# Keeping V on the chip, one K buffer per batch, queries stored once, first heads loaded behind the stores (layers 1 and 4), and a feed-forward with its factors four times

## What is computed

```
# attention of layers 1 and 4, for each batch and head
q = split_heads(ln(x) @ Wq.T + bq) ; k = split_heads(ctx @ Wk.T + bk) ; v = split_heads(ctx @ Wv.T + bv)
p = softmax(q @ k.T / sqrt(8), masked)                 # 256 x 1601
x = x + merge_heads(p @ v) @ Wo.T + bo

# feed-forward of layer 4, rank 32, inner width 512
P = ln(x) @ U1                                         # 128 -> 32
H = gelu(P @ V1 + b1)                                  # 32 -> 512
x = x + (H @ U2) @ V2 + b2                             # 512 -> 32 -> 128
```

## Time and profile before

| | |
|---|---|
| Median of 3 runs | 2220.75 us (2220.43 to 2221.65) |
| The profiled execution's own time | 2221.38 us |
| Its span in the trace | 2219.6 us |
| TensorE busy | 1937.4 us, 87% |
| VectorE busy | 1311.8 us, 59% |
| ScalarE busy | 1287.8 us, 58% |
| DMA queue of SP | 60673 packets, 99.71 MB, 15.0% of 16 engines |

### The profile page before, as it was taken

One profiled execution on the slowest core, in us unless ns is written; L12 is line 12 of the kernel. 1 busy time (PEld: TensorE's weight loads), 2 busy tenths in 40 slices (PEclk: granted clock), 3 DMA queues, 4 the chain that ended last, 5 costly groups with the idle time before them and its releaser, 6 DMA issues. The chain is left out here.

```text
span 2219.6 us, 43657 instructions
## 1 busy us (share of the span) xinstructions
PE 1937.4 (87%) x17168; PEld 1364.1 (61%) x17168; DVE 1311.8 (59%) x3235; ACT 1287.8 (58%) x2062; POOL 130.5 (6%) x352
## 2 busy tenths in 40 slices
PE   5799999956839459999999999999993599999997
PEld 4577777733715356777777777777761356666663
DVE  5688888867446325455455455545546576666652
ACT  3699999943319114555555555555552366666662
POOL 3000000000014110000000000000000300000000
PEclk9899999976959679999999999999995789999996
DMA  7312111101061330000000000000001721112110
GB/s 264 115 54 57 55 54 54 49 16 68 1 174 33 111 113 1 1 1 1 1 1 2 1 1 1 1 2 1 2 1 57 252 68 53 53 56 61 51 32 14
DMA packets 62490, 107.27 MB, mean 48 GB/s; under 512 B 11241, under 2 KB 36541, under 8 KB 62289
## 3 DMA queue, kind: packets, MB, share of 16 engines
q1 hardware_dynamic: 60673, 99.71, 15.0%
q0 software_dynamic: 1616, 4.79, 0.7%
HBM read 75.09 MB, written 29.36 MB: 47 GB/s over the span
## 5 line engine op out<-in xcount | busy, mean ns | idle before, releaser
L2406 ACT ACTIVATE a_prT<-bank 128x512 f32<-128x512 f32 (+1 forms) x448 | 232.7, 565 | 328.3 <-PE bank L2315 328.0
L1212 DVE CUSTOM_DVE_ANT_0 a_attn_junk<-wide,a_mask 128x801 f32<-128x801 f32 (+1 forms) x256 | 247.5, 991 | 124.8 <-PE wide L1043 124.3
L1155 ACT ACTIVATE a_attn_prT<-bank 128x512 f32<-128x512 f32 (+1 forms) x448 | 237.3, 566 | 122.4 <-PE bank L1060 109.7
L2431 DVE CUSTOM_DVE_ANT_0 a_sc<-wide,a_zeros 128x1024 f32<-128x1024 f32 (+1 forms) x256 | 243.1, 987 | 91.9 <-PE wide L2301 91.9
L1501 DVE CUSTOM_DVE_ANT_0 a_attn_sc<-wide,a_mask 128x801 f32<-128x801 f32 (+1 forms) x256 | 252.8, 988 | 14.4 <-PE wide L1355 12.7
L1371 PE MATMUL bank<-ident,a_attn_sc 128*128 128x128 f32 x1664 | 244.4, 275 | 15.2 <-ACT a_attn_prT L1460 14.1
L1371 PEld LDWEIGHTS bank<-ident,a_attn_sc 128*128 128x128 f32 x1664 | 198.1, 141 | 62.6 <-issue 42.5
L2315 PE MATMUL bank<-ident,a_sc 128*128 128x128 f32 x1664 | 231.3, 277 | 1.5 <-ACT a_prT L2406 1.5
L2315 PEld LDWEIGHTS bank<-ident,a_sc 128*128 128x128 f32 x1664 | 185.4, 141 | 54.4 <-issue 28.1
L1466 ACT ACTIVATE a_attn_sc<-a_attn_sc,a_attn_nmx 128x1601 f32<-128x1601 f32 x128 | 209.6, 1638 | 5.7 <-DVE a_attn_nmx L1507 5.6
L2301 PE MATMUL wide<-a_kT,a_qT 64*128 64x512 f32 (+1 forms) x1024 | 211.0, 529 | 0.0
(11 more groups left out here) (456 smaller groups left out, 2561.5 us busy)
## 6 DMA issues: line engine op xcount, KB each, us to landing
a_ks<-a_k_parts SPq DMA_DIRECT2D x384, 75.0 KB
a_k_parts<-a_proj_kp SPq DMA_DIRECT2D x24, 416.0 KB, 5.3
a_v_rows<-a_proj_vb SPq DMA_DIRECT2D x8, 936.0 KB, 6.2
a_vs<-a_v_rows SPq DMA_DIRECT2D x32, 234.0 KB
a_q_stack<-a_proj_qp SPq DMA_DIRECT2D x18, 256.0 KB, 3.8
a_qx<-a_q_stack SPq DMA_DIRECT2D x128, 36.0 KB
moe_w1b<-in_e_w SPq DMA_DIRECT2D x15, 256.0 KB, 2.8
ctxT<-in_ctxT SPq DMA_DIRECT2D x4, 832.0 KB, 10.9
```

The lines of the kernel that those rows point to most:

```text
L1155: act.activation(prT[0:keys, u % PRT, kt:kt + m, :], bank_of(s, f"W{g}")[0:keys, 0:m * S].rearrange("p (t q) -> p t q", q=S), ACT.Exp).the ...
L1212: dve.tensor_tensor_reduce(junk[:, n % 2, 0:w], S_WIDE[n % 2][:, 0:w], mask(qt, at, w), 1.0, LOWEST, ALU.add, ALU.max, mx[:, p % 2, qt, e, ...
L2406: copy = lambda out, src: act.activation(out, src, ACT.Copy)
L2431: dve.tensor_tensor_reduce(sc[:, s % 2, h, at:at + w], S_WIDE[h][:, 0:w], zeros[:, 0:w], 1.0, LOWEST, ALU.add, ALU.max, mx[:, s % 2, h, p: ...
```

## The change

Layers 1 and 4:

- V is copied out of PSUM straight into `vs`, which now holds all four batches and 16 heads, and stays there. `vb`, the V stores, the V loads and TensorE's wait for them are gone. The ones beside V are set by GpSimd (one memset of 832 elements in each partition), not by VectorE (416).
- `kp` has a buffer for each of the four batches; ScalarE's wait for stores is gone.
- Each query part is stored once (three stores, not nine); the load of a head repeats it three times, with one DMA for each part. A head takes six DMAs instead of four.
- The heads 0 and 1 are loaded at the end of the projection block, behind the last K stores on SP, once the stores of the queries and of batch 0 have landed; the attention begins with head 2.

Layer 4's feed-forward: U1 comes four times side by side, so `pT` holds four copies at partitions 0, 32, 64 and 96. V1's four pieces lie at these four, and each matmul of a half uses its own 32 rows of the array and its own bank. The U2 matmuls no longer accumulate: each writes its own 32 partitions of one bank, and V2, four times below itself, sums the four in a contraction over 128. Signals are now one for each half, and a half is finished before the next one's U2 matmuls.

```diff
 def project_stage(...)
-        kp = core.sb(ctx, name + "_kp", [P, 2, 3, cols], BF16)
-        vb = core.sb(ctx, name + "_vb", [P, 2, HEADS, kts * VCOLS], F32)
+        kp = core.sb(ctx, name + "_kp", [P, blocks, 3, cols], BF16)
...
         def _(sp):
             sp.wait_ge(qpart3, 2)
             for j in range(3):
-                for i in range(3):
-                    sp.dma_start(q_rows(j, i), qp[:, j, :]).then_inc(q_stored, 16)
+                sp.dma_start(q_rows(j), qp[:, j, :]).then_inc(q_stored, 16)
             for i in range(blocks):
-                sp.wait_ge(v_evac, ng * (i + 1))
-                sp.wait_ge(ones_in, 1)
-                sp.dma_start(v_rows(i), vb[:, i % 2, :, :]).then_inc(v_stored[i], 16)
                 sp.wait_ge(part3, n_ck * (i + 1))
                 for rows, j in k_rows(i):
-                    sp.dma_start(rows, kp[:, i % 2, j, :]).then_inc(k_stored[i], 16)
-            sp.wait_ge(q_stored, 16 * 9)
+                    sp.dma_start(rows, kp[:, i, j, :]).then_inc(k_stored[i], 16)
+            sp.wait_ge(q_stored, 16 * 3)
+            sp.wait_ge(k_stored[0], 16 * len(k_rows(0)))
+            load_first(sp)
...
             def first_part(n):
-                if i >= 2 and n % n_ck == 0:
-                    act.wait_ge(k_stored[i - 2], 16 * len(k_rows(i - 2)))
...
         def _(pool):
+            pool.memset(vs[:, :, :, :].rearrange("p k h (t d) -> p (k h t) d", d=VCOLS)[:, :, 8:9], 1.0).then_inc(ones_in, 1)
...
         def _(dve):
-            dve.memset(vb[:, :, :, :].rearrange("p k h (t d) -> p (k h t) d", d=VCOLS)[:, :, 8:9], 1.0).then_inc(ones_in, 1)
...
-                        if i >= 2 and c == 0:
-                            dve.wait_ge(v_stored[i - 2], 16)
-                        out = vb[:, i % 2, :, kt * VCOLS:(kt + size) * VCOLS].rearrange(...)
+                        out = vs[:, i, :, kt * VCOLS:(kt + size) * VCOLS].rearrange(...)
 def masked_head_layer(...)
+        def load(sp, b, h, k, sem):
+            for j in range(3):
+                sp.dma_start(ks[24 * j:24 * (j + 1), k, 0:SC],
+                             k_parts[b, h, :, :, 0:SC].rearrange("i d c -> (i d) c")).then_inc(sem, 16)
+            for j in range(3):
+                sp.dma_start(qx[24 * j:24 * (j + 1), k, :],
+                             q_stack[h, j, :, b * S:(b + 1) * S].unsqueeze(0).broadcast_to([3, 8, S])).then_inc(sem, 16)
+        def load_first(sp):
+            for h in range(LOADED_AHEAD):
+                load(sp, 0, h, h, loaded[h])
...
-            sp.dma_start(qx[0:STACK, k, :], q_stack[h, :, :, :, b * S:(b + 1) * S].rearrange("j i d c -> (j i d) c")).then_inc(sem, 16)
 def row_quad_stage(...), quad_attention_stage(...)
-            for u in range(UNITS):
+            for u in range(LOADED_AHEAD, UNITS):
...
-                    pe.wait_ge(v_loaded[q % V_RING], 16 * (q // V_RING + 1))
 def ffn3_stage(...)
+        p_bank, h_bank = bank[0:2], (bank[2:6], bank[6:8] + bank[0:2])
+        q_bank, o_bank = bank[2:4], bank[4:6]
+        rows = lambda i: slice(i * RANK, (i + 1) * RANK)
...
             for c in range(2):
                 pe.wait_ge(p_out, c + 1)
                 for i in range(NC):
-                    if c:
-                        pe.wait_ge(gelu_done, i + 1)
-                    pe.matmul(bank[2 + i][:, :], v1[:, i * P:(i + 1) * P], pT[:, half(c)],
-                              start=True, stop=True).then_inc(h_ready, 1)
+                    ins = pe.matmul(h_bank[c][i][:, :], v1[rows(i), :], pT[rows(i), half(c)], start=True, stop=True)
+                ins.then_inc(h_ready, 1)
             for c in range(2):
                 pe.wait_ge(gelu_done, NC * (c + 1))
                 for i in range(NC):
-                    ins = pe.matmul(bank[c][0:RANK, :], u2[:, i, :], hT[:, c, i, :], start=(i == 0), stop=(i == NC - 1))
+                    ins = pe.matmul(q_bank[c][rows(i), :], u2[:, i, :], hT[:, c, i, :], start=True, stop=True)
                 ins.then_inc(q_ready, 1)
-            for c in range(2):
                 pe.wait_ge(q_out, c + 1)
```

More of the change, by code:

```diff
@@ L893, in _ @@
             for c in range(2):
-                pe.matmul(bank[c][0:RANK, :], u1, core.xnT[:, half(c)], start=True, stop=True).then_inc(p_ready, 1)
+                pe.matmul(p_bank[c][:, :], u1, core.xnT[:, half(c)], start=True, stop=True).then_inc(p_ready, 1)
             for c in range(2):
@@ L960, in quad_attention_stage @@
      recip_done, normed, mixed, mixed_out, out_ready, added, setup) = (core.sem(f"{name}_{s}") for s in names)
-    loaded = [core.sem(f"{name}_loaded{i}") for i in range(RING)]
-    v_loaded = [core.sem(f"{name}_v_loaded{i}") for i in range(V_RING)]
     S_WIDE, BANKS, U_BANK = core.wide, core.bank[0:3], core.bank[3]
@@ L1036, in score_piece @@
                 if n == 0:
-                    pe.wait_ge(loaded[s % RING], 64 * (s // RING + 1))
+                    pe.wait_ge(loaded[s % RING], 96 * (s // RING + 1))
                 if 4 * s + n >= 2:
@@ L1559, in project_stage @@
     k_stored = [core.sem(f"{name}_k_stored{i}") for i in range(blocks)]
-    v_stored = [core.sem(f"{name}_v_stored{i}") for i in range(blocks)]
     K_BANK, V_BANK, Q_BANK = core.bank[0:3], core.bank[3:6], core.bank[6:8]
@@ L1725, in masked_head_layer @@
         qx = q_words[:, :].bitcast(BF16).rearrange("p (s c) -> p s c", s=RING)
-        vs = sb("vs", [P, V_RING, 4, KT * VCOLS])
+        vs = sb("vs", [P, B, HEADS, KT * VCOLS])
+        loaded = [core.sem(f"{name}_loaded{i}") for i in range(RING)]
         mask_in = core.sem(name + "_mask_in")
```

83 lines of the change are left out of this document (32 added, 51 removed).

## The result

| | changed kernel | before, same chip |
|---|---|---|
| median | 2189.1 us (4 runs, 2186.7 to 2189.7) | 2221.2 us (4 runs, 2220.4 to 2224.4) |
| profiled execution | 2189.70 us, span 2187.9 | 2221.38 us, span 2219.6 |

What follows compares the result with a forecast made beforehand. Stores were taken to bound layer 1's projections (layer 4 has the same stages), TensorE the last feed-forward. 17.5 (layer 1) + 13.9 (layer 4) + 15.0 (feed-forward) = 46.4 us gained, giving 2174.4 us; range 2168 to 2183.

Steps and rivals of the forecast that it cites:

- ScalarE's wait goes, the last stores come 13.04 us earlier.: Layer 1's projections: without the wait for K stores, batch 3 and the last K stores come 13.04 us earlier, at 43.0.
- Three took 1.14 us, with the gaps between them I take 0.4 each, 4.8 in all.: End of the projections: SP issues twelve loads before the block can end, 0.4 us each, 4.8 in all.
- the change of block: From projections to attention: 0.5 us allowed, a choice between 0 and 1.
- The bound of 13 for layer 1: Layer 1's projections, forecast gain 17.5 us: lower bound, no gain beyond the 13.04 us by which the last stores move.
- its bound of 11: Layer 4's projections: lower bound of the forecast gain of 13.9 us; the upper was 15.5.
- Layer 4: VectorE's memsets late next: Layer 4's attention start: VectorE's memsets end 2.05 us after the block opens, and its first maximum can't come before.
- Edits at nothing: Layers 1 and 4: memset moved to GpSimd, six DMAs a head; taken as 0, bounds -0.4 to +0.8 us.
- rival 4: Attention of both layers: heads' loads fall behind, slower than before; 2302 us at 1 us per unit; chance 0.03.
- The feed-forward, 15.0: Last feed-forward: packed V1 and U2 matmuls gain 15.0 us if TensorE's clock is at its upper level by 2195.
- rivals 1 and 3: Feed-forward: TensorE's clock stays low, 2178.2 us, chance 0.20; strips of 32 rows don't run together, 2186.6 us, chance 0.06.
- the reason given for the clock: Feed-forward: it goes like layer 1's projections, which begin with two matmuls of U1's shape; upper level before U2, 8 us in.
- rival 1: Feed-forward: TensorE's clock stays at its lower level, 3.8 us more, 2178.2 us; chance 0.20.

Runs made afterwards that it cites:

- after_again: The changed kernel run once more with no edit; 2190.1 us (5 runs, 2185.0 to 2190.9).
- mask_last: The changed kernel with the whole mask work of layers 1 and 4 behind VectorE's last chunk of the last batch; 2185.7 us.
- one_q_load: The changed kernel, but queries stored three times and each loaded with one DMA of 72 rows; 2180.2 us, ratio 0.981.
- ahead1: The changed kernel with only the first head, not two, loaded ahead of the attention block; 2180.4 us, ratio 0.981.
- ff_only: The kernel before with the new last feed-forward alone, nothing changed in layers 1 and 4; 2206.3 us, ratio 0.9925.
- ff_u1_wide_v1_narrow: The changed kernel with the old feed-forward, U1 at 128 columns, V1's matmuls reading 32 rows as before; 2198.8 us, one run.
- ff_first_product_wide: The changed kernel with the old feed-forward, U1 at 128 columns and V1 padded with zeros to 128 rows; 2190.8 us, one run.

## Why the prediction was wrong, step by step

1. **ScalarE's wait goes, the last stores come 13.04 us earlier.** Right in kind. 43.97 instead of 43.0 in layer 1, and 43.23 in after_again, so most of that 1.0 is scatter. In layer 4 the last parts are 1.7 us late, counted from the stage's own start, because batch 3 waits behind the mask instructions (mask_last: 2.7 us of that layer).
2. **"Three took 1.14 us, with the gaps between them I take 0.4 each, 4.8 in all."** This step failed. The price of a key load in an empty queue was put on the query loads, whose form was new, and on loads queued behind stores. Measured 8.7 and 8.4 us: 2.2 of the difference from query loads at 0.69 instead of 0.36 us, 1.6 from the first three behind the stores. one_q_load and ahead1 take SyncE's time away in two different ways, and each gives back 9 us of the kernel's time, 8.4 and 7.3 of it in the two layers' profiles. The sum for layer 1: 1.0 for the parts, 3.9 for the loads, 0.3 for the change of block (0.75 instead of 0.5), and 5.2 is what TensorE's start missed (55.65 for 50.4). In layer 4 it is 1.7 for the parts, 3.6 for the loads and 0.4 for stores and block, and VectorE's first maximum is 5.6 us late; the attention behind it took 0.9 us less than before.
3. **The range.** The bound of 13 for layer 1 let the last stores move and nothing else; it did not hold issue at the largest price that a row shows for one (1815 ns in the old load's row above). 12.4 was measured at TensorE's start and 11.7 at the stage's end; layer 4's 9.1 lies below its bound of 11 too. Even the execution that lost nothing in the untouched stages, 2185.0 us in after_again, lies above the range.
4. **Layer 4: VectorE's memsets late next.** Right: TensorE starts at 1756.80, and the first maximum follows the memsets at 1758.72, 2.0 us after the block's opening.
5. **Edits at nothing.** Right in the main: the attention took 0.7 us longer in layer 1, inside the bounds of -0.4 to +0.8, and 0.9 less in layer 4, outside them. The cover for six DMAs a unit held: in all of both layers TensorE waits for a query load once each, at the start. So rival 4 (slower) did not come.
6. **The feed-forward, 15.0.** Right in size, 15.2, and in ff_only too; rivals 1 and 3 failed. But the reason given for the clock does not hold. I argued from the projections' two matmuls "of the very shape that U1 now has". ff_u1_wide_v1_narrow has them, and the clock stayed at 0.50 for 18 us behind them. So the size was right by luck in this part: if my reading of the strips holds, it was V1's place on four strips that kept rival 1 away, which the argument didn't use. No run shows that.
7. **What nobody had in the sum:** the untouched stages, 4.3 us. after_again shows that it is which way an execution goes, not the change. Its profile gained 36.4 us, 12.6 + 8.7 + 15.2 and -0.1 between. Whether the new start times make the costly way likelier is open: of nine runs of the changed kernel six lie at 2188.7 or above and three at 2186.9 or below.

On the clock, the Trainium skill ("TensorE: Matmul & The Clock Gate", section "What's actually happening") says that activity releases the throttle, and counts the engine busy or idle. The last pair of runs speaks against that reading more sharply than the earlier trace rows did: in the windows shown both kernels keep TensorE at 4.00 of 4.00 us busy, the one at 1.00, the other at 0.50.

The same page of the Trainium skill, section "Measured speedup vs the span model", gives 3.07 times for four row strips of 512 columns. Here a matmul on four-byte floats is two passes. The last two passes of four strips start 0.43 us apart, at 2175.69 and 2176.12, and single passes of 512 columns at the same clock follow at (2172.90 - 2171.18) / 4 = 0.43 in ff_first_product_wide. By the time from start to start, on this one interval, that is four times, not three.

## What to carry to other kernels

When loads are moved ahead of a barrier, the engine that issues them becomes part of the path: price every DMA by its own form, and look for that form's duration in the trace before giving it a neighbour's. Put ahead of the barrier only what fits the issuer's gap, and ask of each wait at a block's end who needs it so soon; here nobody needed the last stores' landing for three heads.

## What the runs showed of the hardware

- A load of 24 rows whose source repeats 8 rows three times took 0.69 us of issue in 384 cases; one of 72 rows took 0.36 in 128, and one of 24 rows of keys 0.36 in 384 (medians).
- The first three key loads behind stores took 2.0 to 3.0 us to issue (1.68 once, 1.4 us behind them), and the first three after a block's opening 1.1.
- Two GpSimd subtractions of 128x416 took 1.91 us by themselves and 2.37 beside a VectorE mask instruction of 128x1068.
- With TensorE busy without a gap, 96 rows of zeros under V1 went with a granted clock of 1.00 instead of 0.50, and 8.6 us of the stage (39.8 to 31.2), in one run of each.
- The clock in layer 2 goes one of two ways in executions of one and the same program: its self-attention took 130.0 us in one and 125.6 in the other, with no edit between.
